# Attention stage of a fused kernel: transposes three heads behind the scores instead of two, weighing four behind instead of three

## What is computed

```python
q = _rope(_rmsnorm(q, q_norm_w), pos)
k = _rope(_rmsnorm(k, k_norm_w), pos)
kc = k_cache[block_table].reshape(bsz, L, HK, D)      # L = 512, HK = 8, D = 128
vc = v_cache[block_table].reshape(bsz, L, HK, D)
k_all = jnp.concatenate([kc, k], axis=1)              # 544 keys
v_all = jnp.concatenate([vc, v], axis=1)
scores = jnp.einsum('bqhd,bkhd->bhqk', q, k_all) * SCALE
scores = jnp.where(valid[:, None, None, :], scores, -1e+30)
probs = jax.nn.softmax(scores, axis=-1)
o = jnp.einsum('bhqk,bkhd->bqhd', probs, v_all)
```

## Time and profile before

| what | value |
|---|---|
| median of three runs | 2338.12 us (2337.94 to 2339.78) |
| the profiled execution | 2333.55 us |
| its span, first to last instruction | 2331.7 us |
| attention stage: start of the first and of the last head's scores | 738.0 and 1952.3 us |
| TensorE busy, whole span | 96% |
| VectorE, ScalarE, GpSimd busy | 76%, 57%, 50% |

### The profile page before, as it was taken

One profiled execution on the slowest core, in us unless ns is written; L12 is line 12 of the kernel. 1 busy time (PEld: TensorE's weight loads), 2 busy tenths in 40 slices (PEclk: granted clock), 3 DMA queues, 4 the chain that ended last, 5 costly groups with the idle time before them and its releaser, 6 DMA issues. The chain is left out here.

```text
span 2331.7 us, 52504 instructions
## 1 busy us (share of the span) xinstructions
PE 2248.5 (96%) x16512; PEld 1950.0 (84%) x16512; DVE 1760.6 (76%) x3503; ACT 1331.9 (57%) x2643; POOL 1161.4 (50%) x1218
## 2 busy tenths in 40 slices
PE   7998999999994999999999999999999997999999
PEld 6877777777773999999999999999999996888887
DVE  8851788888884999999999999999999996422222
ACT  6833888888873666666665666666666654311111
POOL 4200444544543777777777777777777773000000
PEclk9999999999996999999999999999999998999999
DMA  7633343443436888888888888888888885643442
GB/s 264 211 109 104 91 129 112 132 129 124 126 113 214 284 293 295 291 294 293 288 286 285 289 288 294 291 294 292 294 295 289 288 294 172 206 133 95 137 129 63
DMA packets 451815, 501.72 MB, mean 215 GB/s; under 512 B 95861, under 2 KB 390773, under 8 KB 443414
## 3 DMA queue, kind: packets, MB, share of 16 engines
q1 hardware_dynamic: 414870, 366.44, 49.7%
q0 software_dynamic: 36864, 134.23, 16.3%
HBM read 408.21 MB, written 92.34 MB: 215 GB/s over the span
## 5 line engine op out<-in xcount | busy, mean ns | idle before, releaser
L1120 POOL TENSOR_TENSOR att_probs<-att_probs,att_inverse 128x512 f32<-128x512 f32 x512 | 535.1, 1045 | 268.6 <-DVE att_inverse L1316 263.9
L1224 ACT ACTIVATE att_probs<-att_probs,att_low 128x544 f32<-128x544 f32 x512 | 383.8, 750 | 474.2 <-DVE att_low L1303 401.0
L1181 PE MATMUL att_o<-att_probs_t,att_values 128*128 128x128 f32 x4096 | 547.3, 277 | 0.0
L1181 PEld LDWEIGHTS att_o<-att_probs_t,att_values 128*128 128x128 f32 x4096 | 497.4, 192 | 8.6 <-issue 0.2
L1303 DVE CUSTOM_DVE_ANT_0 att_probs<-att_score,att_mask,att_batch_cols 128x544 f32<-128x544 f32 x512 | 398.5, 778 | 74.7 <-PE att_score L1151 55.9
L1312 DVE COPY att_probs_t<-att_turn 128x512 f32<-128x512 f32 x512 | 350.6, 685 | 1.2 <-PE att_turn L1161 1.2
L1106 POOL DMA_INDIRECT att_values<-L_cond_v_cache,att_v_rows_of x256 | 298.3, 1165 | 82.5 <-POOL att_v_rows_of L1102 50.1
L1279 DVE TENSOR_TENSOR att_keys_lo<-att_keys_raw,att_keys_hi 128x480 fp32r<-128x480 f32 (+1 forms) x320 | 321.5, 1006 | 17.4 <-ACT att_keys_hi L1217 17.4
L1161 PE MATMUL att_turn<-ident,att_probs 128*128 128x128 f32 x2048 | 311.2, 274 | 1.2 <-POOL att_probs L1120 0.8
L958 POOL TENSOR_TENSOR proj_q_out<-proj_by_cos,proj_by_sin 128x512 f32<-128x512 f32 x128 | 188.1, 1470 | 216.5 <-DVE proj_by_sin L886 216.5
L1161 PEld LDWEIGHTS att_turn<-ident,att_probs 128*128 128x128 f32 x2048 | 241.7, 141 | 27.7 <-POOL att_probs L1120 1.4
(11 more groups left out here) (129 smaller groups left out, 3920.9 us busy)
## 6 DMA issues: line engine op xcount, KB each, us to landing
att_keys_raw<-L_cond_k_cache SPq DMA_DIRECT2D x1024, 128.0 KB
q_t<-proj_q_out SPq DMA_DIRECT2D x32, 1024.0 KB, 5.3
att_queries_raw<-q_t SPq DMA_DIRECT2D x64, 512.0 KB
o_t<-att_heads_out SPq DMA_DIRECT2D x64, 512.0 KB, 7.8
out_o_raw<-o_t SPq DMA_DIRECT2D x32, 1024.0 KB, 5.8
maps_even<-L_cond_weight SPq DMA_DIRECT2D x8, 1024.0 KB, 12.6
maps_odd<-L_cond_weight SPq DMA_DIRECT2D x8, 1024.0 KB, 16.9
w_nat<-L_cond_Wq SPq DMA_DIRECT2D x8, 1024.0 KB, 6.4
```

Source lines behind the costliest of these rows:

```text
L1120: nc.gpsimd.tensor_tensor(probs[:, k, 0:L], probs[:, k, 0:L], inverse[:, k:k + 1].to_broadcast([P, L]), ALU.mult).then_inc(probs_ready, 1)
L1181: last = nc.tensor.matmul(o, values[j][:, t, h * D:(h + 1) * D], probs_t[m % 2][:, t * P:(t + 1) * P], start=(t == 0), stop=False, skip_gr ...
L1224: nc.scalar.activation(probs[:, k, :], probs[:, k, :], ACT.Exp, bias=low[k][:, 0:1], scale=-1.0, accum_out=total[k][:, 0:1]).then_inc(exp_ ...
```

## The change

TensorE now does `scores(n)`, `turn(n - 3)`, `weigh(n - 4)` in step n, and everything that is tied to these moves along: VectorE's copies (`main_part`) by one step, ScalarE's `new_part` from steps 1 and 5 to steps 2 and 6 and its `keep_o` from steps 2 and 6 to steps 3 and 7, GpSimd's gathers from steps 3 to 6 to steps 4 to 7. No buffer changes its size, no instruction is added or taken away in the steady loop. The cut diff:

```diff
+    LAG = 3
@@ gpsimd
-                    if 3 <= h < 3 + PPT and not (last_pair and j == 1):
-                        if h == 3 and (j or not first):
+                    if 4 <= h < 4 + PPT and not (last_pair and j == 1):
+                        if h == 4 and (j or not first):
                             pool.wait_ge(o_done, i * N + j * HK)
-                        load((j + 1) % 2, i * 2 + (j + 1), h - 3)
+                        load((j + 1) % 2, i * 2 + (j + 1), h - 4)
@@ tensor
                     scores(i, n)
-                    if n >= 2 or not first:
-                        turn(i, n - 2)
-                    if n >= 3 or not first:
-                        weigh(i, n - 3)
+                    if n >= LAG or not first:
+                        turn(i, n - LAG)
+                    if n > LAG or not first:
+                        weigh(i, n - LAG - 1)
@@ scalar
-                    if n % GH == 1 and (n >= GH or not first):
-                        new_part(i, n - 2, first)
                     if n % GH == 2 and (n >= GH or not first):
-                        keep_o(i, n - 3)
+                        new_part(i, n - LAG, first)
+                    if n % GH == 3 and (n >= GH or not first):
+                        keep_o(i, n - LAG - 1)
@@ vector
-                    if n >= 2 or not first:
-                        main_part(i, n - 2)
+                    if (n >= LAG or not first):
+                        main_part(i, n - LAG)
```

More of the change, by code:

```diff
@@ L1203, in _ @@
                 pair(i, False)
[L1204 to L1207, removed]
+            for n in range(-LAG, 0):
+                turn(PAIRS, n)
+                weigh(PAIRS, n - 1)
             weigh(PAIRS, -1)
@@ L1347, in _ @@
             pair(PAIRS - 1, False, True)
-            main_part(PAIRS, -2)
-            main_part(PAIRS, -1)
+            for n in range(-LAG, 0):
+                main_part(PAIRS, n)
 def stage_output(nc, wo, ident, ot_dram, x3_dram, out):
```

## The result

| | before | after |
|---|---|---|
| median of four runs | 2338.03 us | 2355.89 us |
| span of the profiled execution | 2331.7 us | 2351.0 us |
| scores of the first and of the last head start | 738.0, 1952.3 us | 739.2, 1969.3 us |
| step 0 of TensorE, transposes to weighing | 0.43 us | 0.70 us |
| one batch, head 3's scores to head 3's scores | 18.93 us | 19.17 us |

The ratio is 1.0077, 95% interval [1.0059, 1.0094]. The predicted time was 2360, the measured one 2355.9. Between the first and the last scores it is 15.9, and that is the batch: 0.24 x 63 = 15, with the rest in a few longer batches.

A forecast was written before the change was run, and what follows sets the result against it. TensorE was taken as the bound, VectorE second. The batch was to grow from 18.93 to 19.28 us, +0.35 times 63 = +22 us on 2333.55; with the median 4.6 above, 2360 us, range 2341 to 2368.

The forecast's parts named there:

- What bounds the kernel: TensorE, busy for all of a window, then VectorE; waits of 0.32 us per batch, 20 us in 63, could return.
- Transposes one step later: TensorE, step 6: about 2.1 us more slack behind GpSimd's product, so the wait of 0.16 us per batch goes.
- The first gather behind the group, and the splits behind it: GpSimd and VectorE: head 4's product at 6.72, masks of heads 7 and 0 at 10.75 and 13.36 behind head 3's scores.
- `keep_o` in step 7: ScalarE's late result copy: step 0's weighing not before 13.55; wait 0.28 instead of 0.06 us, with 0.10 behind it.
- The split of step 0: VectorE's split meets head 7's product and was taken to end behind the following group: 0.36 us, bounds 0 and 0.36.
- That rival: Step 0's split goes ahead of the GpSimd group: batch 19.08, +8 us, 2346 us; chance 0.2.
- M1: Start of VectorE's mask of head 1, counted from head 3's scores; predicted at 16.16 us.
- Waits go and none comes: Rival: TensorE's 0.32 us per batch returns without new waits, 20 us, 2318 us; chance 0.12.
- M7: Start of VectorE's mask of head 7, counted from head 3's scores; predicted at 10.75 us.

The follow-up runs named there:

- e3_index_early: Changed kernel with GpSimd's copy of the four gather indices one step earlier, ahead of head 3's product; gathers stay in steps 4 to 7: 2320.52 us.
- e9_no_split_lag3: Changed kernel with VectorE's subtractions of key and query halves left out, lo halves filled with zeros instead: 2319.19 us.
- e10_no_split_lag2: Kernel before with VectorE's subtractions of key and query halves left out, lo halves filled with zeros instead: 2328.83 us.
- e2_keep_first: Changed kernel with ScalarE's copy of the four results (keep_o) ahead of the key part of its step instead of behind it: 2356.22 us.
- e1_gathers_alone: Kernel before with only GpSimd's gathers moved to steps 4 to 7, transposes still two heads behind: 2434.92 us.
- e5_lag_alone: Changed kernel with GpSimd's gathers put back in steps 3 to 6, transposes three heads behind: 2428.88 us.

## Why the prediction was right, and where not

- *What bounds the kernel.* Right. TensorE's own batch is 18.62 us in four different kernels with three heads of lag, and the changed kernel's 19.17 is that plus waits at the places named. By the medians over the batches it loses against e3_index_early 0.09 up to the scores of head 0 (those of head 7 wait for the mask before them), 0.35 at the weighing of step 0 and 0.11 behind the scores of head 2, 0.55 in all.
- *Transposes one step later.* Right: step 6 is at 0.84, and e9_no_split_lag3 against e10_no_split_lag2 shows a gain of 9.6 us from lag when nothing is stopped.
- *The first gather behind the group, and the splits behind it.* Right to 0.02 us for head 4's product and the masks of heads 7 and 0. TensorE's scores of heads 7 and 0 were walked at 9.2 and 11.9 and came at 9.11 and 11.81, because head 7's follow the mask before them by 0.82 and not by 0.85 to 0.94; the copy of the results hid that. The two runs that take this meeting apart from either side (e3_index_early, e9_no_split_lag3) give back 35 and 37 us: the loss of 18 us and most of the 20 us of waits that the kernel before had.
- *`keep_o` in step 7.* The wait was sized right (weighing at 13.55, measured 13.54). As a cause it was put beside the other, and e2_keep_first shows that taking it away alone brings nothing, for the mask of head 1 is as late. In the prediction's sum the two were chained by the later one too, so the sum did not count it twice.
- *The split of step 0.* Wrong. I took the group to go ahead of the waiting split, by the row of the first stage, and gave the other order 0.2. In 62 of 64 batches the split goes first. This is what the Trainium skill's rule on who issued first (page "SBUF — State Buffer", section "Who interferes with whom") gave, and here the trace agrees: split issued at 1418.17, group at 1418.75, and the group takes 1.00. It does not agree everywhere: in e1_gathers_alone a split that begins at 1477.89 stands through a product that begins at 1478.38. The row that I leaned on shows another instruction, a copy with one input, which had begun before both sums (32.44 against 32.58) and still ended behind them. The term was 0.36 and should have been 0. The prediction named this as a sign that the forecast is wrong, a split that ends 0.69 behind head 7's product, and the sign came (0.70), though the time of 2346 that it put beside it did not.
- *Why the sum held all the same.* Partly by luck. That rival's own batch was 19.08 and its time 2346. Two terms that it lacked bring it to 19.17. The last gather took 1.39 instead of the 1.22 that I used for all, so head 7's product ended at 15.28, M1 came at 15.97, and head 2's scores just touched that bound (16.79, free 16.80). And scores that wait for their mask, or follow the new keys' products with raw heads, take 1.02 to the transposes instead of 0.92; I had no such term. 0.10 per batch is 6 us. So the batch gave 15 us and a few longer ones 1, where the sum had 22; 3.4 us outside the scores, which the sum had at nothing (1.2 ahead of the stage, 2.2 behind its last scores), made up over half of the difference. The median was forecast 4 us too high. In the sum itself the low end of the batch, 19.24, does not come out of its own terms: 16.16 - 0.02 + 0.85 + 2.28 = 19.27.
- *Waits go and none comes.* Its deciding point, M7 below about 10.47, can be checked: in e3_index_early M7 is at 10.20, and the time is 2320.5 for 2318 predicted under that rival.

## What to carry to other kernels

When the tuned order of one engine is shifted against another by a step, walk one period of every engine with the durations of the trace, and look for where two instructions that exclude each other will now overlap; the waits of the bound engine tell only what lag can return, here 20 us, not what the new meetings cost. Ahead of a row of instructions without slack, move out what need not stand there: a copy of four indices with its 0.77 us of idle behind it was worth 35 us. And a wait that is removed shows its worth only if the next one behind it is not as late.

## What the runs showed that I had not expected

- Between a GpSimd product and the group that follows it without a gap, a waiting VectorE subtraction gets in (62 of 64 second groups of the changed kernel, 1.00 instead of 0.40 for the group). Behind a gather it is otherwise: in e1_gathers_alone a subtraction that starts at 1477.89, 0.52 into a gather, stands through the gather's end and the whole product that follows, 2.07 in all. In e3_index_early one that starts 0.10 into a gather runs free in 0.65 and is over 0.25 before the product. All traces with splits together divide cleanly: of the 382 subtractions that start inside a gather (three of them of 640 columns, the rest of 480), the 261 whose next product begins 0.80 or more behind their start run free, and the 121 whose next product begins 0.50 or less behind it (54 of them in e1_gathers_alone, 62 in e5_lag_alone) stand through that product. Why the product that begins later goes first stays open; no run separates the gather's last part from the product that follows it.
- The subtractions hold up the gathers too. Gathers that begin while a split is still running take 1.22 or 1.39 in the changed kernel and end 0.85 to 0.88 behind that split's end; without splits (e9_no_split_lag3) the second to fourth gathers take 0.98. That is where the 1.39 of the last gather comes from: the split of 640 columns ahead of it ends 0.53 into the gather, one of 480 columns 0.37.
- A GpSimd copy of four columns waits for a VectorE subtraction that began before it: 0.61 against 0.18 us.
- Matmuls that had to wait cost about 0.1 us more than the wait: 1.16 for 1.06 in a weighing, 1.02 for 0.92 from raw scores to transposes (the second also behind the new keys' products, where nothing is waited for: 1415.33 to 1416.36 in the changed kernel, 1.03).
